# Third expert layer's front: first-choice rows weighed and added by GpSimd, second-choice rows by VectorE behind it

## The reference, cut to what matters

```python
x = x + 0.5 * _L0_ffn_ref(_layernorm(x), ...)      # every token: two experts, two weights
x = x + 0.5 * _L1_ffn_ref(_layernorm(x), ...)

# _L0_ffn_ref: sum over the two chosen experts of w_e * (silu(a) * b @ W2_e + b2_e)
# _L1_ffn_ref, xf being the normalised x:
logits = xf @ router_w.T
probs = jax.nn.softmax(logits, axis=-1)
k_probs, k_idx = jax.lax.top_k(probs, K)           # K = 2 of E = 8
k_probs = k_probs / jnp.sum(k_probs, axis=-1, keepdims=True)
...                                                # rows to experts, capacity, silu, back
return combined.reshape(B, T, H) + x               # x here is the normalised x
```

## Time and profile before

| | |
|---|---|
| median of three executions | 3465.14 us |
| the profiled execution, its own time | 3467.05 us |
| span of the profile | 3465.1 us |
| mean granted TensorE clock | 0.906 of full |
| PE, PE's weight loads | 2665.2 us (77%), 1899.1 us (55%) |
| VectorE (DVE) | 2212.2 us (64%) |
| ScalarE (ACT) | 1566.1 us (45%) |
| GpSimd (POOL) | 2013.3 us (58%) |

### The profile page before, as it was taken

One profiled execution on the slowest core, in us unless ns is written; L12 is line 12 of the kernel. 1 busy time (PEld: TensorE's weight loads), 2 busy tenths in 40 slices (PEclk: granted clock), 3 DMA queues, 4 the chain that ended last, 5 costly groups with the idle time before them and its releaser, 6 DMA issues. The chain is left out here.

```text
span 3465.1 us, 43989 instructions
## 1 busy us (share of the span) xinstructions
PE 2665.2 (77%) x12436; PEld 1899.1 (55%) x12436; DVE 2212.2 (64%) x4048; ACT 1566.1 (45%) x2687; POOL 2013.3 (58%) x1639
## 2 busy tenths in 40 slices
PE   5788886997688888547888678878887876497773
PEld 4677775444577777536778223333332324386663
DVE  6655554787754555684233499999999997832223
ACT  5333333775633333333233566767676654332221
POOL 0466663232056666424564389999999785156665
PEclk9999998999699999759999799999999998698886
DMA  6111111110411111341223488889888884222223
GB/s 177 43 39 40 41 40 42 41 33 1 128 36 41 38 40 40 92 125 47 68 71 65 144 294 295 288 301 303 282 296 302 294 300 152 66 65 65 75 72 82
DMA packets 287328, 429.80 MB, mean 124 GB/s; under 512 B 59197, under 2 KB 196800, under 8 KB 287201
## 3 DMA queue, kind: packets, MB, share of 16 engines
q1 hardware_dynamic: 251744, 357.54, 31.5%
q0 software_dynamic: 35456, 70.86, 8.7%
HBM read 367.71 MB, written 62.39 MB: 124 GB/s over the span
## 5 line engine op out<-in xcount | busy, mean ns | idle before, releaser
L709 POOL DMA_INDIRECT m_rows<-rows_in,m_source x568 | 554.0, 975 | 651.7 <-SPq L606 209.4
L763 PE MATMUL m_Y_ps<-m_own,m_hid 128*128 128x128 f32 x4544 | 590.9, 285 | 226.8 <-DVE m_hid L848 101.0
L763 PEld LDWEIGHTS m_Y_ps<-m_own,m_hid 128*128 128x128 f32 x4544 | 554.2, 199 | 252.7 <-DVE m_hid L848 111.9
L1635 POOL TENSOR_TENSOR s_dBu<-s_du,s_B_row 128x1024 f32<-128x1024 f32 x256 | 602.3, 2359 | 127.2 <-DVE s_dA L1958 77.4
L1670 PE MATMUL s_y_ps<-s_prod,ident 128*128 128x512 f32 x1024 | 522.5, 636 | 188.5 <-DVE s_prod L1965 188.5
L1958 DVE TENSOR_TENSOR_SCAN s_dA<-s_dA,s_dBu 128x1024 f32<-128x1024 f32 x256 | 585.5, 2287 | 6.3 <-ACT s_dA L1775 6.3
L747 PE MATMUL m_A_ps<-m_rowsT,m_own 128*128 128x256 f32 x2272 | 580.4, 389 | 6.2 <-issue 4.4
L799 ACT ACTIVATE m_act_a<-m_A_ps,m_own 128x256 f32<-128x256 f32 x568 | 231.7, 473 | 532.3 <-PE m_A_ps L747 477.5
L747 PEld LDWEIGHTS m_A_ps<-m_rowsT,m_own 128*128 128x128 f32 x2272 | 423.2, 197 | 57.2 <-issue 6.9
L1670 PEld LDWEIGHTS s_y_ps<-s_prod,ident 128*128 128x128 f32 x1024 | 182.4, 196 | 494.9 <-DVE s_prod L1965 290.3
L716 POOL DMA_INDIRECT rows_by_token<-m_y_sb,m_target x284 | 311.9, 1098 | 243.7 <-DVE m_y_sb L858 173.4
(11 more groups left out here) (251 smaller groups left out, 3647.8 us busy)
## 6 DMA issues: line engine op xcount, KB each, us to landing
s_B_row<-s_bc_rows SPq DMA_DIRECT2D x256, 512.0 KB
s_C_row<-s_bc_rows SPq DMA_DIRECT2D x256, 512.0 KB
rows_out<-m_y_sb SPq DMA_DIRECT2D x142, 128.0 KB
rows_in<-m_xs SPq DMA_DIRECT2D x64, 256.0 KB, 2.3
m_rows<-rows_in,m_source POOLq DMA_INDIRECT x568
s_got<-rows_by_token SPq DMA_DIRECT2D x16, 512.0 KB
m_got<-rows_by_token SPq DMA_DIRECT2D x32, 256.0 KB, 4.1
rows_by_token<-m_y_sb,m_target POOLq DMA_INDIRECT x284
```

The lines of the kernel that those rows point to most:

```text
L709: pool.indirect_dma_start(rows[:, b % AHEAD, r, :], None, c.rows_in, bass.IndirectOffsetOnAxis(source[:, 2 * b + r:2 * b + r + 1], 0)).the ...
L763: ins = nc.tensor.matmul(Y_ps[slot][:, r, :], hid[:, slot, f, at(r, P)], own[:, slot, W2 + f * D:W2 + (f + 1) * D], start=(f == 0), stop=( ...
L1635: nc.gpsimd.tensor_tensor(dBu[q % RING][:, :], du[s % 2][:, h, :], B_row[q % RING][:, :], ALU.mult).then_inc(dBu_ready, 1)
```

## The change

VectorE no longer adds the first-choice rows. GpSimd does, a whole group (512 columns) at a time and in two instructions: the first multiplies the fetched rows in place by the weights, which are broadcast over the features, the second adds them to x; a new semaphore stands between the two (`first_scaled`), and another (`first_added`) tells VectorE. VectorE's four additions of the second-choice rows wait for it. GpSimd's own-x instructions (`add_own`) now come four groups late: behind `add_first` of group g stands `add_own` of group g-4. `rows_added` now counts 4 a group in place of 8, and the waits on it are changed to match. Where there are no rows before (`m3`), the order of `add_own` is what it was.

```diff
--- before.py
+++ after.py
@@ -266,7 +266,7 @@
             root_ready, scale_step, scales_ready = rsem("root_ready"), rsem("scale_step"), rsem("scales_ready")
             self_added = rsem("self_added")
             rows_here = [rsem(f"rows_here{u}") for u in range(4)]
-            rows_added = rsem("rows_added")
+            first_scaled, first_added, rows_added = rsem("first_scaled"), rsem("first_added"), rsem("rows_added")
             high_ready, low_ready, rows_coded = rsem("high_ready"), rsem("low_ready"), rsem("rows_coded")
             tiles_coded = rsem("tiles_coded")
             marks_used = rsem("marks_used")
@@ -283,19 +283,16 @@
                 gain, guard = (1.0 + RMS_EPS, RMS_EPS * LN_EPS) if gated else (1.0, LN_EPS)
 
                 def add_rows(g):
-                    dve.wait_ge(rows_here[g % 4], (g // 4 + 1) * 32)
-                    for k in range(2):
-                        if k == 1:
-                            dve.wait_ge(rows_added, g * 2 * GRP + GRP)
-                        for j in range(GRP):
-                            t = g * GRP + j
-                            nc.vector.scalar_tensor_tensor(
-                                out=c.x[:, at(t), :], in0=got[:, g % 4, k, j, :].unsqueeze(1), scalar=weight[k][:, at(t)],
-                                in1=c.x[:, at(t), :], op0=ALU.mult, op1=ALU.add).then_inc(rows_added, 1)
+                    for j in range(GRP):
+                        t = g * GRP + j
+                        dve.wait_ge(first_added, t + 1)
+                        nc.vector.scalar_tensor_tensor(
+                            out=c.x[:, at(t), :], in0=got[:, g % 4, 1, j, :].unsqueeze(1), scalar=weight[1][:, at(t)],
+                            in1=c.x[:, at(t), :], op0=ALU.mult, op1=ALU.add).then_inc(rows_added, 1)
 
                 def statistics(g):
                     if rows_before:
-                        dve.wait_ge(rows_added, (g + 1) * 2 * GRP)
+                        dve.wait_ge(rows_added, (g + 1) * GRP)
                     elif c.x_loaded is not None:
                         dve.wait_ge(c.x_loaded[g // 2], 16)
                     for t in range(g * GRP, g * GRP + GRP):
@@ -564,16 +561,32 @@
             def _(pool):
                 if ahead is not None:
                     ahead.clear()
-                if not gated:
-                    for t in range(NT):
+                def add_first(g):
+                    pool.wait_ge(rows_here[g % 4], (g // 4 + 1) * 32)
+                    nc.gpsimd.tensor_tensor(got[:, g % 4, 0, :, :], got[:, g % 4, 0, :, :],
+                                            weight[0][:, at(g, GRP)].unsqueeze(2).to_broadcast([P, GRP, D]),
+                                            ALU.mult).then_inc(first_scaled, 1)
+                    pool.wait_ge(first_scaled, g + 1)
+                    nc.gpsimd.tensor_tensor(c.x[:, at(g, GRP), :], c.x[:, at(g, GRP), :], got[:, g % 4, 0, :, :],
+                                            ALU.add).then_inc(first_added, GRP)
+
+                def add_own(g):
+                    for t in range(g * GRP, g * GRP + GRP):
                         pool.wait_ge(scales_ready, (t // (2 * GRP) + 1) * 3)
                         pool.wait_ge(xs_ready, t + 1)
                         nc.gpsimd.tensor_scalar(c.x[:, at(t), :], c.x[:, at(t), :], own_gain[:, at(t)], own_shift[:, at(t)],
                                                 ALU.mult, ALU.add).then_inc(self_added, 1)
+                if not gated:
+                    OWN_LAG = 4
+                    for g in range(NG + OWN_LAG):
+                        if rows_before and g < NG:
+                            add_first(g)
+                        if g >= OWN_LAG:
+                            add_own(g - OWN_LAG)
             @block.sync
             def _(sp):
                 def fetch(g):
-                    wait(sp, rows_added, (g - 3) * 2 * GRP)
+                    wait(sp, rows_added, (g - 3) * GRP)
                     for k in range(2):
                         sp.dma_start(got[:, g % 4, k, :, :], c.rows_by_choice[k].rearrange("(t p) d -> p t d", p=P)[:, at(g, GRP), :]
                                      ).then_inc(rows_here[g % 4], 16)
```

## The result

The median went from 3464.38 to 3476.10 us (20 executions each, on the chip of the front's profile): +11.7 us, ratio 1.003 with a 95% interval of 1.0023 to 1.0038, which is +8.0 to +13.2 us. The profiled execution took 3476.12, span 3474.1. Forecast were +16.5 and 3481.6.

The account below looks back on a forecast made before the run. The prediction took a closed loop from fetched rows through scales and store to the next fetch, in the third expert layer's front, as the bound; start 6.0, five turns 9.0 and tail 1.5 gave +16.5 us, 3481.6, range 3470 to 3492.

Parts of the forecast that it names:

- The bound: Front of the third expert layer: closed loop of additions, scales, normalise, store, fetch and landing, 9.22 us a turn.
- rival C: Front: the ring of four groups covers the landing and GpSimd paces; -3.7 us, 3461.4, chance 0.06.
- GpSimd's pair, 2.72 us: GpSimd's two 128x512 instructions a group: 2 x 1.27, plus 0.08 gap, plus 0.1 until VectorE sees it.
- The turn, +1.80: One loop round between landed rows of even groups: +1.72 to the reciprocal, +0.08 for scales; 9.0 us in five.
- The start, +6.0: Groups 0 to 3, fetched ahead: GpSimd runs eight instructions back to back, holding VectorE's additions; first spread +6.0 us.
- Rival A: Front: GpSimd and VectorE do not exclude each other with these operands; +10.1 us, 3475.2, chance 0.20.
- The tail, +1.5: From the rows of group 14: GpSimd's pairs and own-x delay group 15's additions, +2.75 - 1.25 = +1.5 us.
- The own-x backlog: Tail: own-x additions of groups 11 to 15, 20 x 0.55 = 11 us, hidden before `chosen` by 9 us.
- Rival B: Loop turns: GpSimd's multiplication of the odd group catches the scales, +1.3 more a turn; +23 us, 3488, chance 0.15.
- Rival D: Behind the front: code position makes the 9.4 us stop near 1598.6 go or double; 3472 or 3490, chance 0.09.
- The sum: Whole kernel: 6.0 + 9.0 + 1.5 = +16.5 us, giving 3481.6 us.

Follow-up runs that it names:

- e1: Kernel before, with SyncE issuing the fetches of groups g+4 and g+5 ahead of the store of even group g: 0.9955, then 0.9979 of the kernel before.
- e2: Changed kernel with SyncE's fetches issued early, ahead of the store: 0.9998 of the kernel before, front 88.25 us.
- e4: Changed kernel with GpSimd's two instructions for odd groups only, VectorE adding both choices of even groups: 0.9997 of the kernel before, front 93.41 us.
- e3: Changed kernel; for groups 1 to 3 GpSimd first waits until VectorE has added the second choice of the group before: 1.0022 of the kernel before.
- e6: Changed kernel with VectorE's additions reading constants from a PSUM bank instead of second-choice rows: rows of group 4 after 17.24 us, turns 11.84 us.

## Why the prediction was right, and where it was off

**The bound: right.** e1 shows that the front was a closed loop through SyncE's order, and e2 and e4 that the price depends on being in it. That rival C could not happen with this order is shown by the 1.6 us for which GpSimd still waits each turn.

**GpSimd's pair, 2.72 us: too large by 0.24.** It took 2.48 (1451.24 to 1453.72). The addition is the interpolated 1.27; the broadcast multiplication is 1.04, the operand to which I gave no price. The 0.1 until VectorE sees the signal rested on no row; here VectorE starts 0.04 behind the addition's end, and the gap inside the pair is 0.14 for the 0.08 forecast.

**The turn, +1.80: mis-sized, +1.27 measured.** 0.24 is the multiplication. The four additions to the reciprocal took 1.13 instead of 1.23: with own-x beside them all four last 1.21, for 1.13 alone (group 2), so that company costs 0.08 and not 0.15. The scales beside GpSimd cost 0.02 more and not 0.08. Of the remaining 0.13, 0.09 lies in the mean of before, which holds one late landing (9.22 for the usual 9.13). That GpSimd would wait for rows and not pace the front was right.

**The start, +6.0: right in its mechanism, +4.4 measured.** The additions of group 0 were held (341, 1116 and 1345 ns as least, median and most of the four), as only e3 and e6 prove. But the step that every GpSimd instruction lets only one addition through was too slow: they start at 1432.95, 1433.98, 1434.24 and about 1435.5, so between the end of the second multiplication and the data of the dependent addition VectorE got two through, and the group was done at 6.2 us behind the first landing instead of 8.4. The forecast also let the statistics run from 1439.5, where its own last addition ends at 1439.8; as GpSimd's end at 1442.2 ruled from there, nothing hangs on it. Rival A, without exclusion, had +0.7 here and is refuted.

**The tail, +1.5: mis-sized, +0.5.** The additions of group 15 start 6.89 us behind the rows of group 14, where 7.9 was forecast: two pairs at 2.43 and 2.48 for 2.7 each, four own-x at 1.98 for 2.1, and no hold for 0.3. The softmax instruction beside GpSimd's multiplication lasted 0.72, and held GpSimd's addition by nothing (1.27). The own-x backlog, 20 instructions in 9.8 us, was hidden as forecast.

**Rival B** did not occur in the changed kernel, by a margin of about 0.2 us: the last scale instruction ran from 1455.25 to 1455.41 and GpSimd's multiplication started at 1455.64. That is close: it came out by the sizes, and I can't claim to have forecast 0.2 us. e4 and e6 are what it looks like.

**Rival D** is refuted as a cause. On the first chip ScalarE's stop is there in both traces:

```profile
1598.63 1.09 ACT L804 ACTIVATE m_hid<-m_A_ps 128x512 f32<-128x512 f32 x2 [9.41 <-remote]
```

```profile
1608.82 1.08 ACT L817 ACTIVATE m_hid<-m_A_ps 128x512 f32<-128x512 f32 x2 [8.43 <-remote]
```

It changes by 1 us. (GpSimd's own idle time there is 2.64 us, not the 9.4 that the prediction gave to both.) And none of the eleven traces from the other chips has a single wait that the profile calls remote, while the front there loses the same 10.8 us. Why engines stop so on the first chip stays open.

**The sum** was 16.5 for 11.2 in the trace and 11.7 in the medians. Every step had the right sign and an engine's name that the trace confirms; all three terms were too large, so none made up for another. That the measured time lies in the range says little by itself, since rival A's 3475.2 lies in it too.

## What to carry to other kernels

Busy shares make GpSimd look like free room; ask first whether the work to be moved lies between a transfer's landing and the next request for one, and look whether the request could simply be issued earlier, which here gave -8.5 us of front for five new lines. Then ask what the helper takes from the engine it helps: GpSimd beside VectorE on SBUF operands gave back what it took (1.16 for 1.16 us), while with ScalarE writing to PSUM neither engine's instructions became longer and a turn fell from 7.88 to 6.85. A short instruction that others wait for is the one to keep clear of a long GpSimd one.

## What the runs showed of the hardware that I had not expected

- VectorE's tensor_scalar with a single SBUF input is held too, for 1.26 us instead of 0.17 beside a GpSimd addition (e3), and own_gain (0.16 elsewhere) lasted 0.36 in e6. I had reckoned with two-input instructions only. The Trainium skill, "SBUF — State Buffer", section "SBUF: two separate sides", names VectorE instructions in a two-port mode beside those with two SBUF inputs; that fits, but no run here shows in which mode this one ran. Statistics instructions beside the same GpSimd instructions kept their 0.87 for four.
- GpSimd's two-input instruction on 512 columns takes 1.04 us with a broadcast operand and 1.26 with two dense ones, for multiplication and addition alike where dense.
- Waiting goes both ways at once: GpSimd's addition in the start lasted 1.38 instead of 1.26, and its four own-x instructions 2.0 beside SBUF additions but 1.74 beside those from PSUM.
